# Four empty instructions behind each gather of a product-key lookup, in an audio tower on one core

## The reference, cut to what matters

```
qh = (q_tok @ Wq.T + bq).reshape(-1, H, 2, HALF)          # H = 8 heads
sub_scores = einsum('nhcf,hcef->nhce', qh, keys)          # 128 keys in each half
s, idx = top_k(sub_scores, 8)
best_s, best_pos = top_k(s[..0] + s[..1], 8)              # 8 of the 64 pairs
indices = take_along_axis(all_idx, best_pos)              # 8 heads x 8 rows per token
x = gelu(einsum('nd,nhkd->nhk', q_tok, w_down_embed[indices]))
out = einsum('nhk,nhkd->nd', x * softmax(best_s), w_up_embed[indices])
```

## Time and profile before

| | us |
|---|---|
| median of three timed runs | 3447.02 |
| lowest, highest | 3434.35, 3462.33 |
| span of the profiled execution | 5577.0 |
| its busy time: PE, DVE, ACT, POOL | 3254.3, 2619.7, 2226.7, 2330.6 |

### The profile page before, as it was taken

How to read it: one execution, slowest core, us unless ns; L and a number is a source line. 1 busy time by engine, 2 the same in 40 slices (tenths; PEclk the granted TensorE clock), 3 DMA queues, 4 the chain that set the end, 5 groups by cost and what they waited for, 6 DMA issues and landing times. The chain is left out here.

```text
span 5577.0 us, 53095 instructions
## 1 busy us (share of the span) xinstructions
PE 3254.3 (58%) x14195; PEld 2193.0 (39%) x14195; DVE 2619.7 (47%) x13857; ACT 2226.7 (40%) x4627; POOL 2330.6 (42%) x2451
## 2 busy tenths in 40 slices
PE   4356445556665554655655665656546655665678
PEld 2133233334334333443433434434333433443456
DVE  3443554544454445444543554554435445544633
ACT  2235232234543442344425433543534344344444
POOL 4544444353443444434344434443353444444410
PEclk7556677676777776787767777777767777776879
DMA  5223224142332432243233324333332333343320
GB/s 172 89 80 105 69 81 136 55 118 78 99 95 71 121 91 81 78 120 102 77 101 96 93 76 116 91 90 104 105 90 68 102 97 99 90 116 91 95 79 3
DMA packets 314967, 519.04 MB, mean 93 GB/s; under 512 B 56746, under 2 KB 171308, under 8 KB 314668
## 3 DMA queue, kind: packets, MB, share of 16 engines
q0 software_dynamic: 119808, 316.15, 20.5%
q10 hardware_dynamic: 86784, 130.06, 7.5%
q1 hardware_dynamic: 108076, 69.45, 4.2%
HBM read 498.64 MB, written 11.17 MB: 91 GB/s over the span
## 5 line engine op out<-in xcount | busy, mean ns | idle before, releaser
L766 POOL DMA_INDIRECT ring<-in_table_dram,idx x2432 | 2328.4, 957 | 3015.7 <-PE bank_u L861 1521.4
L1023 PE MATMUL bank_x<-z3t,w_b 128*128 128x255 f32 (+1 forms) x1264 | 425.7, 470 | 410.9 <-ACT eo L3302 194.0
L5409 DVE CUSTOM_DVE_ANT_0 ring<-ring,bank_q 128x128 f32<-128x128 f32 (+1 forms) x2432 | 537.4, 281 | 232.6 <-issue 176.4
L861 PE MATMUL bank_u<-ring,ident 128*128 128x512 f32 (+1 forms) x912 | 543.6, 743 | 151.7 <-ACT ring L3196 66.8
L3196 ACT ACTIVATE ring<-ring,vu 128x128 f32<-128x128 f32 (+1 forms) x1824 | 555.5, 390 | 131.5 <-DVE vu L5415 73.6
L3297 ACT ACTIVATE ht<-bank_x,b_s 128x255 f32<-128x255 f32 (+1 forms) x704 | 289.3, 463 | 657.6 <-remote 404.3
L1026 PE MATMUL bank_x<-ht,w_b 128*128 128x255 f32 (+1 forms) x1264 | 386.7, 459 | 207.5 <-ACT ht L3297 179.3
L1023 PEld LDWEIGHTS bank_x<-z3t,w_b 128*128 128x128 f32 x1264 | 269.4, 236 | 518.0 <-ACT eo L3302 211.8
L1026 PEld LDWEIGHTS bank_x<-ht,w_b 128*128 128x128 f32 x1264 | 283.6, 239 | 295.4 <-ACT ht L3297 197.9
L861 PEld LDWEIGHTS bank_u<-ring,ident 128*128 128x128 f32 (+1 forms) x912 | 206.3, 239 | 392.8 <-issue 280.6
L1070 PE MATMUL bank_x<-qd,tb 128*128 128x128 f32 x1280 | 227.1, 332 | 210.1 <-ACT gs L3227 100.9
(11 more groups left out here) (235 smaller groups left out, 5418.1 us busy)
## 6 DMA issues: line engine op xcount, KB each, us to landing
w_b<-in_w_dram ACTq DMA_DIRECT2D x304, 256.0 KB
ring<-in_table_dram,idx POOLq DMA_INDIRECT x2432
tb<-turned ACTq DMA_DIRECT2D x120, 256.0 KB
tb<-in_table_dram SPq DMA_DIRECT2D x120, 256.0 KB
tb<-turned SPq DMA_DIRECT2D x40, 256.0 KB
tb<-in_table_dram ACTq DMA_DIRECT2D x40, 256.0 KB
gs<-in_table_dram SPq DMA_DIRECT2D x32, 256.0 KB
turned<-gs ACTq DMA_DIRECT2D x32, 256.0 KB
```

The costliest lines, as they stand in the source:

```text
L766: pool.indirect_dma_start(ring[0:rows, u, k, :], None, table, bass.IndirectOffsetOnAxis(ap=idx[0:rows, j, c:c + 1], axis=0)).then_inc(gath ...
L861: ins = mm(U[0:rows, :], ident[0:rows, 0:rows], ring[0:rows, u, 4 * c:4 * c + 4, D:ROW], start=(u == 0 and c == 0), stop=(u == UNITS - 1 a ...
L1023: ins = mm(to[:, m * n:m * n + n], wa[:, k * D:(k + 1) * D], x, start=True, stop=True)
L5409: ins = dve.tensor_tensor_reduce(w, w, qrep[r, b, :], 1.0, 0.0, ALU.mult, ALU.add, xu[r, k:k + 1])
```

## The change

Behind each indirect transfer POOL gets four `engine_nop` instructions. Such an instruction reads nothing, writes nothing and sets no semaphore; the sequencer hands it to the engine, and the engine executes it in its turn. They are 9728 in all, beside the 2451 instructions that POOL has now.

```diff
@@ -766,6 +766,8 @@
                         pool.indirect_dma_start(
                             ring[0:rows, u, k, :], None, table,
                             bass.IndirectOffsetOnAxis(ap=idx[0:rows, j, c:c + 1], axis=0)).then_inc(gathered[u], 16)
+                        for _ in range(4):
+                            pool.engine_nop()
```

## The result

The changed kernel takes 3477.5 us (median of five runs, 3464.63 to 3487.57) against 3447.08 us (median of five). The ratio is 1.0082, with a 95% interval of 1.005 to 1.0115: 0.8% slower, about 28 us, where 9.8% was forecast and 3540 us was the bottom of the range.

A forecast was written before the change was run, and what follows sets the result against it. POOL's gather stream was taken as the bound, PE second. Head 58, stream 3058 plus 389 for the empties, tail 230 and remaining waits 50 gave 3785 us, 9.8% slower; range 3540 to 4340 us.

The forecast's parts named there:

- the standstill: While gathers stream, other engines nearly stop in the 5577 us profile; taken as part of being traced, not in timed runs.
- POOL's rhythm: Gather start to gather start on POOL: 1.25 us, 0.95 busy and 0.30 idle, taken from the trace as valid for timed runs.
- the tail: Stretch behind the last gather, POOL doing nothing: 229.57 us, claimed to stay as it is.
- the price: POOL's time per empty instruction behind a gather: 40 ns, charged in full, 389 us for all 9728.
- The question of cover: Whether the 0.30 us behind each gather hides the empties; claimed to be work that covers nothing, so 389 us stay.
- The bound: POOL's stream of gathers sets the timed kernel, 3346 us or 97% of 3447; PE second at some 2640 us, 77%.
- 50 of 101 us: POOL's waits in a timed run, about 101 us; half was expected to go as slower gathers give other engines time.
- C: Rival: price hidden in the 0.30 us gap, or POOL's true pace is 0.957 us; time stays 3447 us; chance 0.08.
- B: Rival: tracing slows POOL, true pace below 1.25 us, so waits absorb part; about 3600 us; chance 0.13.
- A: Rival: each empty instruction on POOL costs a whole small one, 0.09 us; some 4240 us; chance 0.17.
- D: Rival: wider spacing of gathers frees other engines, shortening POOL's waits at L758 and L762; down to 3346 us; chance 0.04.
- my case: Each empty instruction costs POOL 30 to 60 ns, pace 1.41 us at the forecast; 3640 to 3980 us; chance 0.58.

The follow-up runs named there:

- run 1: The kernel before, unchanged, profiled a second time; its span is 3448.8 us, where the first profiled execution took 5577 us.
- run 2: Sixteen empty instructions behind each gather in place of the changed kernel's four; 4075.32 us, ratio 1.1806 to the kernel before.
- run 5: Three empty instructions behind each gather in place of the changed kernel's four; 3455.47 us, ratio 1.0023 to the kernel before.
- run 6: Eight empty instructions behind each gather in place of the changed kernel's four; 3604.36 us, ratio 1.0447 to the kernel before.
- run 7: The kernel before with a one-element-per-partition memset behind each gather, no empties, and one wait per unit on earlier memsets; 3452.75 us, ratio 0.9994.
- run 8: The kernel before with one gather in sixteen left out from the third tile on, output not the reference's; 3443.82 us, ratio 0.9986.
- run 10: The kernel before with four gathers in sixteen left out from the third tile on, output not the reference's; 3445.19 us, ratio 0.9982.
- run 11: The changed kernel with its four empties only in tiles 3 to 27 (1600 gathers); 3456.25 us, ratio 1.0019 to the kernel before.
- run 12: The changed kernel with its four empties only in tiles 0 to 2 and 28 to 37 (832 gathers); 3466.96 us, ratio 1.0048 to the kernel before.
- run 4: Sequencer nops written in place of the changed kernel's four empties, but absent from the profile; 3449.76 us, ratio 1.000 to the kernel before.

## Why the prediction was wrong, point by point

**Reading the long profile.** The inference that the standstill could not be in a timed run holds. But it was not a matter of being traced either: run 1 was traced and has none. What held the engines in that one execution stays open; it did not come again. Taking only POOL's rhythm from the trace was right for the pace: 1.25 us in both. Two parts of the sum were off in opposite senses: the tail is 178.6 us, not 230, and a gather's mean is 975 ns (2370.47/2432), not 957, since beside busy engines a few are longer. POOL's floor by run 1 is 59 + 2370 + 742 + 179 = 3350 us, against 3346 on record, and its waits are 98 us, against 101. PE, by run 1, is busy 2877 us (83%), not the 2640 (77%) that I scaled it to.

**The change part by part.** Count and place were right: 9728, no other engine's list touched, pace up and the gather's own 0.95 us unchanged. The step that failed is the price. 40 ns each was to be charged in full. An empty takes 20.8 ns, below the nearest row from below (the memsets 0.03 us apart), and the first 67 ns of them behind a gather are free (runs 2, 5, 6). Four therefore cost 15 to 16 ns, not 160: 38 us of stream, not 389. Of the 351 us too many, 187 are the price of one empty (four at 20.8 ns charged in full would be 202 us) and 164 the cover that was put at nothing.

**The question of cover.** I asked it, set the two readings against each other, and chose wrongly to charge everything. "The gap is as long behind 85 rows as behind 128" shows a fixed part; it does not show that nothing else fits inside it. The conclusion that the gap "covers nothing" was mine, and runs 5 and 7 refute it, for a memset too. Nor does the whole gap give cover: of 305 ns, 67 do and 238 do not, and the 238 come after the last empty. What POOL does in either piece, no run here shows. The Trainium skill (Perfetto Trace Analysis, DMA Instruction — SWDGE (GPSIMD)) puts a gather's profiled end at its last descriptor and says that the DSP completes the instruction after that, but not how long this takes or what can run beside it. In the rows the empties start at that very end, so no time of such a completion is seen ahead of them.

**The bound.** "The timed kernel is set by POOL's stream, with PE second" took 97% for a bound. Runs 8 and 10 show that with less load on POOL the time is still 3440 us and more. PE is 83% busy, DVE 74%, and the order among the engines takes the same time. Two limits lie close together here: POOL's own 3350 us and some 3440 us of the others. The traces can be added up (us). The stream is the gathers' busy time and the gaps, those between units at their median; waits are what those gaps have above it.

| | stream | waits | head and tail | span |
|---|---|---|---|---|
| before (run 1) | 3112.5 | 98.4 | 238.0 | 3448.8 |
| four | 3154.6 | 87.8 | 237.5 | 3479.9 |
| eight (run 6) | 3365.2 | 0.1 | 235.2 | 3600.5 |
| sixteen (run 2) | 3836.2 | 1.7 | 236.2 | 4074.0 |
| 15 of 16 (run 8) | 2929.3 | 253.4 | 254.4 | 3437.0 |
| 12 of 16 (run 10) | 2374.3 | 792.8 | 280.5 | 3447.6 |

With eight and sixteen nothing is left of the waits, and the span is head, stream and tail. With four, 42 us of stream took only 11 us out of the waits, although 88 were there, and the rest arrived. So the waits are not one reserve that a longer stream uses up first: they lie in some places, and the stream holds the others up elsewhere. That is the reading that runs 11 and 12 were to test, and they do not settle it; nor is it shown why a longer stream costs at once while a shorter one gains nothing. I let 50 of 101 us go. The change took 11, and a stream 253 us longer took all 98, so this term was mis-sized as well, by less than 50 us against the 350 of the price. With the right price the sum says 3447 us and at most 38 more, up to 3485, which holds the 3477.5. The error that decided was the price.

**The rivals.** C (no effect, the price hidden in the gap) was nearest, at 0.08: the four are four fifths hidden. Its other branch, a true pace of 0.957 us, is wrong. B's cause (tracing slows POOL) is wrong, A's price is over four times too high, and D did not occur: no run is clearly faster than the kernel before. "No engine of rows 1 would fill more than about 80% and 3447 would have no cause" was the weakest argument against C. In run 10 no engine is over 83% busy, POOL is at 52%, and the time is 3445 us all the same: the order among the engines can be a cause with none of them full.

**What was to show it.** The pace at 1.41 us was the test of my case; 1.27 us was measured, near C. The count of 12179 on POOL was wrong, since the profile lists empties on the queue.

## What to carry to other kernels

Before an added instruction is charged in full, ask how much the gap behind its neighbour takes in; a run with many of them gives the slope, and one with few the free part. An engine at 97% of the span need not be the only bound: take work away from it as well as adding some, because a kernel with two limits close together gets slower by the one and no faster by the other. If a profiled span is far from the timed runs, take a second trace before a sum is built on its stretches. And look in a control's profile for the instructions that it is to hold (here the count and the instruction queue's bytes): run 4 looked like a clean result and held none.

## What the runs showed of the hardware that I had not expected

An empty engine instruction on POOL took 20.8 ns from start to start, in rows of 4, 16 and 64. Behind an indirect gather of 0.95 us and a gap of 305 ns, three of them, or one memset of one element per partition, moved the next gather by nothing; the fourth moved it by 15 ns, and further ones by 20.8 ns each. Each empty brought about 64 bytes on the instruction queue. An execution of the same program took 5577 us once under the profiler and 3449 us the next time.
